# Attention with experts on one core: scores placed beside maxima of the other row half, values two steps back, the expert item ahead of the last two scores

## What is computed

```python
x = x + attn(xn) + ffn(xn)
# attn: 16 heads of size 8, keys and values through a latent of 32
q = (x @ Wq + bq); latent = x @ Wl + bl
k = latent @ Wk + bk; v = latent @ Wv + bv
scores = einsum('bihd,bjhd->bhij', q, k) * SCALE      # 1024 x 1024 for each of 2 x 16 heads
out = einsum('bhij,bjhd->bihd', softmax(scores), v) @ Wo + bo
# ffn: 16 experts, the two best of each token, weighed by a softmax over their logits
glu = gate * sigmoid(gate * 1.702); out_e = ((up + 1) * glu) @ Wd + bd
```

## Time and profile before

| | |
|---|---|
| median of 3 runs | 520.67 us (517.59 to 520.69) |
| the profiled execution | 515.9 us, of which the span from the first to the last instruction is 514.0 us |
| mean granted clock of TensorE | 0.913 of 2.4 GHz |
| PE busy | 453.2 us (88%), 2681 matmul records |
| PE weight loads | 209.3 us (41%) |
| DVE busy | 374.6 us (73%) |
| ACT busy | 309.4 us (60%) |
| POOL busy | 192.9 us (38%) |
| DMA | 39.01 MB, mean 76 GB/s |

### The profile page before, as it was taken

The page is one execution under the profiler, slowest core; times in us unless marked ns, Lnnn a source line. Parts: engine busy times, 40 slices in busy tenths (PEclk is TensorE's granted clock), DMA queues, the critical chain, the costliest instruction groups (busy, mean ns, idle before and its releaser), DMA issues.

```text
span 514.0 us, 8995 instructions
## 1 busy us (share of the span) xinstructions
PE 453.2 (88%) x2681; PEld 209.3 (41%) x2681; DVE 374.6 (73%) x725; ACT 309.4 (60%) x356; POOL 192.9 (38%) x240
## 2 busy tenths in 40 slices
PE   0998984998989899989898989898989889799885
PEld 0554441333434344444444444444444434353243
DVE  8479992768888888888888878888888776764011
ACT  1541022477777686768686868686868644448840
POOL 6035876004141414141414141414141461824870
PEclk9976557789999999999999999999999988979966
DMA  8465512500544655304502443041004020101200
GB/s 239 126 120 179 101 44 87 162 3 1 129 123 121 189 102 111 104 1 78 109 22 83 86 100 104 3 82 22 21 3 91 16 59 7 39 22 43 57 23 25
DMA packets 39298, 39.01 MB, mean 76 GB/s; under 512 B 4998, under 2 KB 34792, under 8 KB 38376
## 3 DMA queue, kind: packets, MB, share of 16 engines
q1 hardware_dynamic: 35808, 33.74, 26.3%
q0 software_dynamic: 2432, 4.72, 3.9%
q10 hardware_dynamic: 1032, 0.23, 0.3%
HBM read 23.73 MB, written 13.89 MB: 73 GB/s over the span
## 4 chain that ended last, share of the span: by engine, by line
PE 59%; POOL 11%; DVE 11%; ACT 8%; issue 6%; another core or an unknown queue 2%; DMA 1%; ACTq 0%; SPq 0%; DVEq 0%; POOLq 0%
PE banks L987 17%; PE banks L970 16%; PE banks L1035 11%; DVE half_max L810 7%; ACT probs L674 5%; PE banks L1056 3%; PE banks L1054 3%; POOL th L545 2%; POOL up L546 2%; POOL up L528 2%; PE banks L1019 1%; PE banks L1017 1%; POOL th L544 1%; POOL up L541 1%
## 5 line engine op out<-in xcount | busy, mean ns | idle before, releaser
L810 DVE TENSOR_REDUCE half_max<-banks 128x1 f32<-128x512 f32 x512 | 322.0, 685 | 52.9 <-PE banks L970 39.9
L674 ACT ACTIVATE probs<-banks 128x1024 f32<-128x1024 f32 x256 | 254.9, 1026 | 162.5 <-PE banks L1035 113.1
L970 PE MATMUL banks<-k_rows,q_rows 62*128 62x512 f32 x512 | 182.9, 484 | 14.6 <-DVE half_max L810 10.4
L1035 PE MATMUL banks<-q_rows,k_rows 64*128 64x512 f32 x512 | 141.7, 460 | 7.0 <-ACT probs L674 5.5
L987 PE MATMUL banks<-probs,v_pad 128*32 128x512 f32 x1024 | 142.4, 630 | 0.0
L970 PEld LDWEIGHTS banks<-k_rows,q_rows 62*128 62x128 f32 x512 | 87.9, 199 | 103.5 <-DVE half_max L810 72.0
L1035 PEld LDWEIGHTS banks<-q_rows,k_rows 64*128 64x128 f32 x512 | 63.1, 192 | 77.6 <-ACT probs L674 66.9
L528 POOL TENSOR_TENSOR gate<-gate,w_blk 128x512 f32<-128x512 f32 x12 | 12.6, 1048 | 108.3 <-ACT gate L658 108.3
L528 POOL TENSOR_TENSOR up<-up,w_blk 128x512 f32<-128x512 f32 x12 | 12.6, 1049 | 97.8 <-ACT up L660 97.8
L510 POOL DMA_INDIRECT x_table<-xn,place_u x32 | 31.1, 972 | 20.9 <-DVE place_u L792 11.5
L987 PEld LDWEIGHTS banks<-probs,v_pad 128*32 128x32 f32 x1024 | 20.7, 110 | 44.3 <-issue 35.3
(11 more groups left out here) (117 smaller groups left out, 345.2 us busy)
## 6 DMA issues: line engine op xcount, KB each, us to landing
w_blk<-in_wexp SPq DMA_DIRECT2D x48, 193.0 KB, 3.1
q_rows<-q_parts SPq DMA_DIRECT2D x28, 128.0 KB
k_rows<-k_parts SPq DMA_DIRECT2D x56, 64.0 KB
x_table<-zeros SPq DMA_DIRECT2D x1, 3072.0 KB, 12.5
x_rows<-x_table SPq DMA_DIRECT2D x12, 256.0 KB, 3.7
moe_table<-x_rows SPq DMA_DIRECT2D x12, 256.0 KB, 6.8
q_parts<-q SPq DMA_DIRECT2D x8, 256.0 KB
k_parts<-k SPq DMA_DIRECT2D x8, 256.0 KB
```

Of the source, the lines that this page charges most:

```text
L674: nc.scalar.activation(probs[:, (2 * s + part) % 4, :, :], banks[:, bank:bank + 2, :], ACT.Exp, scale=SCALE).then_inc(slot_free, 1)
L810: nc.vector.tensor_reduce(half_max[:, unit, row, half:half + 1], banks[:, ring_bank(job), :], AX_X, ALU.max).then_inc(ring_free, 1)
L970: pe.matmul(bank, q_rows[slot][rows, pair, q0:q0 + P], k_rows[slot][rows, pair, 512 * keys:512 * keys + 512], start=True, stop=True).then_ ...
L1035: mm = pe.matmul(banks[:, bank + u, :], k_rows[(unit // 2) % 2][rows, pair, P * kb:P * kb + P], q_rows[(unit // 2) % 2][rows, pair, 512 * ...
```

## The change

```diff
 def max_place(n):
-    return n // 16, n // 4 % 4, n // 2 % 2, n % 2
+    return n // 16, n // 4 % 4, n // 2 % 2, 1 - n % 2
+
+def prob_slot(s):
+    return s % 3 if s < STEPS + 2 * HEAD - 2 else (s + 1) % 3
+
+def values_done(s):
+    return s - 2 if s < STEPS + 2 * HEAD - 2 else s - 1
...
-        attnT = sb("attnT", [P, 512])
+        attnT = xT_blk
-        probs = sb("probs", [P, 4, 2, 512])
+        probs = sb("probs", [P, 6, 2, 512])
...
-                        store_max(sp, unit, job_base(t) + jobs_before(p, HEAD, last) + (5 if has_max(p, last) else 0))
+                        store_max(sp, unit, job_base(t) + jobs_before(p, HEAD, last) + 8 * has_max(p, last))
...
             def exps(base, slot, t, s, part):
                 act.wait_ge(slot_full, base + slot + 1)
-                if s >= 2:
-                    act.wait_ge(s_pv, STEPS * t + s - 1)
+                if s >= 3:
+                    act.wait_ge(s_pv, STEPS * t + values_done(s))
...
             def pair(base, slot, t, p, last):
                 exps(base, slot, t, 2 * p, 0)
                 exps(base, slot + 1, t, 2 * p, 1)
+                exps(base, slot + 2, t, 2 * p + 1, 0)
                 if p % 4 == 0 and p > 0:
                     keep_pv(t, p // 4 - 1)
                 if tanh_group(p, last) is not None:
                     tanh_of(t, tanh_group(p, last))
-                exps(base, slot + 2, t, 2 * p + 1, 0)
...
-                mm.then_inc(slot_full, 1)
+                    if u == 1:
+                        mm.then_inc(slot_full, 1)
+                    if maxima:
+                        max_job(jbase, job + 2 * pair + u, s + LEAD, 2 * pair + u)
...
                 a, b = 2 * p, 2 * p + 1
                 maxima = has_max(p, last)
-                scores(sbase, slot, a, 0, t)
-                if maxima:
-                    max_job(jbase, job, a + LEAD, 0)
-                scores(sbase, slot + 1, a, 1, t)
-                if maxima:
-                    max_job(jbase, job + 1, a + LEAD, 1)
-                    max_job(jbase, job + 2, a + LEAD, 2)
+                scores(sbase, slot, a, 0, t, jbase, job, maxima)
                 if p > 0:
-                    values(sbase, slot, t, a - 1)
-                if maxima:
-                    max_job(jbase, job + 3, a + LEAD, 3)
-                scores(sbase, slot + 2, b, 0, t)
-                if maxima:
-                    max_job(jbase, job + 4, b + LEAD, 0)
-                    job += 5
+                    values(sbase, slot - 2, t, a - 2)
+                scores(sbase, slot + 1, a, 1, t, jbase, job, maxima)
+                scores(sbase, slot + 2, b, 0, t, jbase, job + 4, maxima)
+                if p > 0:
+                    values(sbase, slot, t, b - 2)
                 if has_item(p, last):
                     item(sbase, slot + 3, t, *item_of(p, last))
+                scores(sbase, slot + 3 + has_item(p, last), b, 1, t, jbase, job + 4, maxima)
+                if maxima:
+                    job += 8
...
-                if maxima:
-                    max_job(jbase, job, b + LEAD, 1)
-                    max_job(jbase, job + 1, b + LEAD, 2)
-                scores(sbase, slot + 3 + has_item(p, last), b, 1, t)
-                if maxima:
-                    max_job(jbase, job + 2, b + LEAD, 3)
-                values(sbase, slot + 2, t, a)
```

More of the change, by code:

```diff
@@ L312, in moe_attention_kernel @@
         last_jobs = jobs_before(PAIRS, HEAD, True)
-        OUT_JOB = {2 * b + half: jobs_before(p + 1, HEAD, True) + (5 if has_max(p + 1, True) else 0) + turned_jobs(p + 1, True) - 1
+        OUT_JOB = {2 * b + half: jobs_before(p + 1, HEAD, True) + 8 * has_max(p + 1, True) + turned_jobs(p + 1, True) - 1
                    for p, (b, half) in PROJECT.items()}
@@ L670, in exps @@
                 act.wait_ge(slot_full, base + slot + 1)
-                if s >= 2:
-                    act.wait_ge(s_pv, STEPS * t + s - 1)
+                if s >= 3:
+                    act.wait_ge(s_pv, STEPS * t + values_done(s))
                 bank = 2 * (slot % 2)
-                nc.scalar.activation(probs[:, (2 * s + part) % 4, :, :], banks[:, bank:bank + 2, :], ACT.Exp,
+                nc.scalar.activation(probs[:, 2 * prob_slot(s) + part, :, :], banks[:, bank:bank + 2, :], ACT.Exp,
                                      scale=SCALE).then_inc(slot_free, 1)
@@ L694, in _ @@
                     unit = (2 * p + LEAD - 2) // KB
-                    store_max(act, unit, AHEAD_JOBS + jobs_before(p, 0, False) + 5)
+                    store_max(act, unit, AHEAD_JOBS + jobs_before(p, 0, False) + 8)
                     load_max(act, unit, unit + 1)
@@ L856, in pair @@
                 maxima = [(2 * p + LEAD + n // 4, n % 4) for n in range(8)] if has_max(p, last) else []
-                for n, (ahead, m) in enumerate(maxima[:5]):
+                for n, (ahead, m) in enumerate(maxima):
                     max_job(base, job + n, ahead, m)
-                job += len(maxima[:5])
+                job += len(maxima)
                 if has_max_turn(p, last):
@@ L874, in pair @@
                     job += 1
-                for n, (ahead, m) in enumerate(maxima[5:]):
-                    max_job(base, job + n, ahead, m)
             for p in range(HEAD):
@@ L987, in values @@
                     mm = pe.matmul(banks[32 * j:32 * j + 32, 4, :], v_pad[:, (unit // 2) % 2, kb, j, :],
-                                   probs[:, (2 * s + j // 2) % 4, j % 2, :], start=(kb == 0), stop=(kb == KB - 1))
+                                   probs[:, 2 * prob_slot(s) + j // 2, j % 2, :], start=(kb == 0), stop=(kb == KB - 1))
                 mm.then_inc(s_pv, 1)
@@ L1025, in score_slot, with scores @@
                 return 2 * (slot % 2)
-            def scores(base, slot, s, pair, t):
+            def scores(base, slot, s, pair, t, jbase, job, maxima):
                 unit, kb = divmod(s, KB)
@@ L1114, in pair @@
                     project(jbase, job, *PROJECT[p - 1])
-                    job += 1
-                if maxima:
-                    max_job(jbase, job, b + LEAD, 1)
-                    max_job(jbase, job + 1, b + LEAD, 2)
-                scores(sbase, slot + 3 + has_item(p, last), b, 1, t)
-                if maxima:
-                    max_job(jbase, job + 2, b + LEAD, 3)
-                values(sbase, slot + 2, t, a)
             pe.wait_ge(s_place, 1)
@@ L1132, in _ @@
                 pair(jbase, jobs_before(p, HEAD, True), sbase, slots_before(p, HEAD, True), TURNS - 1, p, True)
-            values(sbase, slots_before(PAIRS, HEAD, True), TURNS - 1, STEPS - 1)
+            slot = slots_before(PAIRS, HEAD, True)
+            values(sbase, slot - 2, TURNS - 1, STEPS - 2)
+            values(sbase, slot, TURNS - 1, STEPS - 1)
             job = jobs_before(PAIRS, HEAD, True)
```

## The result

The changed kernel took 540.90 us (median of 4 runs, 536.45 to 541.24), the kernel of before 520.68 beside it (median of 4 runs). The ratio is 1.0375, with a 95% interval from 1.030 to 1.045. The forecast was 537.5. The profiled execution took 540.8 us with a span of 538.9; that of before took 515.9 with a span of 514.0.

A forecast was written before the change was run, and what follows sets the result against it. PE was taken to lead with DVE close behind; cycles +15.6, seams +1.5, ahead of the loop +1 and loads -1 summed to +17, so 533 profiled and, with the 4.8 offset, 537.5 us; range 524 to 552.

The forecast's parts named there:

- (e): Seams of loop bodies: two exps wait for values over a reused probability buffer, +1.5 us (0 to 3).
- (f): Turned maxima go through memory half a pair later: loop cost 0 (slack 0.7), +1 us (0 to 3) ahead of it.
- (g): Last turn: 0, plus or minus 2 us; longer pairs make the group loads late less often, -1 us.
- What bounds it: PE, the matmul engine, leads, busy 77.45 of 82 us, with DVE (VectorE) close behind at 68.31.
- The chain of 1.27: First maximum's start to the fourth's in a stretch, over three banks: 0.54 plus reduction 0.685 plus 0.05, 1.27 us.
- (a): Two four-place stretches of 1.13 a pair, not three: PE alone would need 5.35 us, 0.42 less than 5.77.
- (b): Fourth maximum of a stretch waits for the first's bank, until 1.27: plain pair 6.43 us (6.27 to 6.49), DVE idles 1.1.
- (c): Turns at the pair's end: pairs of 6.96 and 7.12, POOL's 1.03 wait gone; cycle +1.3, twelve cycles +15.6 us.
- (d): ScalarE's work and six probability buffers: no cost or gain; the item copy's wait is hidden, else 0.2 a pair.
- the clock falls: Rival: short PE waits lower the clock in a tenth to a third of pairs, +15 to +48 us more; chance 0.10.
- The pairing pays: Rival: PE leads and having two stretches is what counts; 20 us less, 500 us; chance 0.08.
- A wash: Rival: the old waits in a cycle go and pay for the ring's new ones; 521 to 526 us; chance 0.09.

The follow-up runs named there:

- experiment 2: The changed kernel with each reduction reading only the first 256 of its 512 columns; 521.5 us, ratio 1.010.
- experiment 1: The changed kernel with maxima 5 and 6 moved between the second values and the item, so no stretch has four; 526.5 us, ratio 1.024.
- experiment 4: The kernel of before with values two steps back, six probability buffers, attnT on xT_blk and keep_pv at the pair's end; 517.8 us, ratio 1.004.
- experiment 9: The changed kernel, unaltered, run a second time; 538.2 us, ratio 1.038.
- experiment 10: Changed kernel with maxima 5, 6 and turns ahead of the item, maxima 0, 1 ahead of first scores, POOL splitting maxima before up work; 535.2 us, ratio 1.034.
- experiment 11: The kernel of before with POOL splitting the maxima ahead of the up work; 532.9 us, ratio 1.032.
- experiment 8: The changed kernel with the weights of expert group 2 asked for in pair 9, not pair 7, on SP's queue; 514.2 us, ratio 1.049.

## Why the prediction was right

The mechanism was right. That the total came within 3.4 us is in part luck. The forecast carried an offset of 4.8 us from the profiled execution of before to the median; the changed kernel shows none (540.8 and 540.9). From profile to profile the growth was 24.9 us for the forecast +17. The cycles account for 1.2 of the 8 that are missing; the rest are the terms (e), (f) and (g), which were each too low.

- **What bounds it** held. PE leads before, and in the change the ring of three banks couples it to DVE. The chain of 1.27 was measured as 1.28, and it follows the reduction (1.02 in experiment 2).
- **(a)** PE alone would need 5.35: not seen, as no version was free of the other waits. The stretch of four places between the values was 1.12 in experiment 1 (forecast 1.13). No run sets apart what a change of tiling mode costs.
- **(b)** Plain pair: I took 6.43 from between 6.27 and 6.49; it is 6.51. The 0.43 behind a matmul that waited holds in both stretches. The hole of 1.1 in DVE's work was 1.3.
- **(c)** Turned values 6.74 (forecast 6.96), turned maxima 7.11 (7.12). Cycle: +1.4 (forecast +1.3), so +16.8 for +15.6. The turned maxima didn't wait for POOL, by 0.13 us.
- **(d)** The values' distance is worth nothing in sum: experiment 4. The item's copy, hidden now, was called the next wait; experiment 1 shows it, though at 0.36 and not 0.2.
- **(e)** The seams: the two pairs at the second seam take 15.4 after and 14.1 before, 1.3 more, where the same kinds of pairs elsewhere differ by 0.3. So about 1.0 (1.4 at the first seam) for the 0.5 forecast, and most of it isn't what was forecast. Stretch by stretch, beside the pairs from 233.04 to 246.89: PE does wait 0.47 for an exp that had waited for values, but that stretch is only 0.1 longer, since the ring's wait covers the rest. 0.4 stand ahead of the down item, which waits for POOL, 0.1 go to a wait for k_rows, and 0.4 to the first stretch of the next body, where the ring starts in the bank of the turned maxima. The kernel of before pays 0.2 at its seam. The prediction had no term for the down item's wait or for the ring's.
- **(f)** The turned maxima weren't late in the loop of the changed kernel. They were late once in its last turn (0.68 us at 502.7; 0.88 in experiment 9) and twice in experiment 1: the slack is as thin as said. Ahead of the loop +3.3 for +1; 1.2 of it is there at the first turn of the maxima (66.5 and not 65.3), and the first maximum already starts 2.0 later (43.4 and not 41.4; 42.0 in experiment 9), before anything of the new order.
- **(g)** was wrong in sign for the loads. I expected the group loads to be late less often (-1), but PE waited 4.2 us for k_rows, in five places, and 0.3 before. The step overlooked that a pair's boundary now comes sooner behind its item: PE needed the rows 15.4 us behind the gate item of two pairs earlier and not 15.9, and in the first body SP had issued them 0.3 later. That explains the three waits of 0.3, not the 2.24. It varies, though: 3.0 in experiment 9. The last turn took +1.0 for the forecast 0.

Of the rivals, "the clock falls" is excluded by 1.00 in the loop. Past the first pair of the loop, long records (the lower level) stand only behind waits such as the 1.18 and the 4.71 above, in every profile, and not behind each such wait: behind the 2.24 in the changed kernel the values took 1.07. What the Trainium skill tells under psum-queue depth-cycling (TensorE: Matmul & The Clock Gate), a clock that swings when PE idles briefly and often between its groups, found no counterpart here for waits of 0.2 to 0.5 us. "The pairing pays" failed at its condition: the fourth maximum waits 0.48. "A wash" failed since the turn's place gave back what it saved.

## What to carry over

Before instructions are regrouped on an in-order engine, count in each stretch between two large blocks how many users of a ring stand in it: the one beyond the ring's size waits for a whole round of the consumer, and everything behind it waits too. Removing the first wait shows the next one, so a forecast for a mended version needs all of them: here the ring, the slot of the item, POOL's chain and the way through memory lay within about a microsecond of each other. One period of a loop is not enough: twice (experiments 10 and 11) an edit made each cycle about 1 us faster than before and lost it at the seams and in the last turn. And a ring whose size does not divide the jobs of a body has a tighter place at the seam.

## What the runs showed of the hardware that was not expected

The kernel of before had a median of 491 us in one group of runs and of 514 to 521 in the others. The record lists the group with 491 and that with 517 under one chip number, so what differed isn't known. The changed order took the same time in the loop to 0.4 us (320.6 and 321.0, experiments 8 and 9). The whole difference lay in the parts ahead of it and behind it, and these ran at different granted clocks: from 80 to 95 us 0.99 in experiment 8 and 0.52 in experiment 9, and in the first 24 us behind the loop 1.00 and 0.86 (over the whole execution 0.948 and 0.911). Why the clock differed wasn't found. A change in the loop therefore reads as a larger ratio in the group in which the rest is shorter.

The loads of the same q and k rows came at different times in two executions of the same kernel: PE's waits for k_rows added up to 4.2 us in five places in the first profile of the changed kernel and to 3.0 in four places in the second, and its longest, 2.24, was missing in the second. Over the profiles of all versions the sum ran from 0.3 to 10.2 us.
